# Expert routing inside the gating stage with bf16 masks, and unread products between the layers' matmuls

## The reference, cut to what matters

```python
x = x + attn(layernorm(x))            # 4 layers, width 128, hidden 512: "the layers"
x = x + xattn(layernorm(x), ctx)      # a gate per channel, from the context's greatest values: "the gating"
x = x + ffn(layernorm(x))             # 8 experts, the best 2 for each token: "routing" and "the experts"
```

```python
gate_logits = einsum('bsh,he->bse', x, gate_w)
top_vals, top_idx = top_k(gate_logits, 2)
probs = softmax(top_vals)
out = sum over the two experts e of a token: probs[e] * (x @ expert_w[e])
```

## Time and profile before

| | us |
|---|---|
| runs, median of 3 (lowest, highest) | 1199.26 (1190.36, 1199.87) |
| the profiled execution's own time | 1194.41 |
| its span, first to last instruction | 1192.4 |
| start and embedding, to the first `z` of the layers | 0 to 124.66 |
| layers, slots s = 0 to about 15 | 124.66 to 412 |
| end of the layers, gating | 412 to 615 |
| routing | 615 to 655 |
| experts | 655 to 1192 |

### The profile page before, as it was taken

How to read it: one execution, slowest core, us unless ns; L and a number is a source line. 1 busy time by engine, 2 the same in 40 slices (tenths; PEclk the granted TensorE clock), 3 DMA queues, 4 the chain that set the end, 5 groups by cost and what they waited for, 6 DMA issues and landing times. The chain is left out here.

```text
span 1192.4 us, 13599 instructions
## 1 busy us (share of the span) xinstructions
PE 1042.3 (87%) x3593; PEld 575.2 (48%) x3594; DVE 570.3 (48%) x1637; ACT 393.8 (33%) x1124; POOL 487.3 (41%) x661
## 2 busy tenths in 40 slices
PE   6786888888888869989965699999999999999995
PEld 6784454454544435425965344444444444444442
DVE  5636479788888677996965211111111111211111
ACT  2435778676756316866830000000000000000000
POOL 3834467546655201005710643333444333334431
PEclk9878899888889979988765799999999999999998
DMA  8310110110000123000795247354645636374432
GB/s 304 121 54 0 46 68 13 54 36 1 1 1 1 70 79 134 1 1 18 283 350 215 73 86 226 74 177 104 211 79 136 169 73 211 70 211 82 86 78 36
DMA packets 38462, 120.27 MB, mean 101 GB/s; under 512 B 6219, under 2 KB 9350, under 8 KB 38406
## 3 DMA queue, kind: packets, MB, share of 16 engines
q1 hardware_dynamic: 25590, 79.77, 18.1%
q0 software_dynamic: 12816, 39.86, 15.4%
HBM read 82.91 MB, written 36.70 MB: 100 GB/s over the span
## 5 line engine op out<-in xcount | busy, mean ns | idle before, releaser
L1952 PE MATMUL bank<-T,X 128*128 x1184 | 510.6, 594 | 13.9 <-DVE X L1990 10.8
L1952 PEld LDWEIGHTS bank<-T,X 128*128 128x128 f32 x1184 | 225.2, 191 | 298.6 <-issue 298.6
L2004 DVE TENSOR_SCALAR X<-bank,col_p 128x512 f32<-128x512 f32 x37 | 27.8, 750 | 410.5 <-PE bank L1952 410.5
L1970 ACT ACTIVATE X<-bank,col_p 128x512 f32<-128x512 f32 x37 | 25.4, 687 | 523.2 <-PE bank L1952 523.2
L1905 POOL DMA_INDIRECT X<-x_nrm,col_s x156 | 149.5, 958 | 92.9 <-issue 46.9
L1914 POOL DMA_INDIRECT out_dram<-X,col_d x37 | 60.0, 1622 | 268.6 <-DVE X L2004 255.0
L450 POOL TENSOR_TENSOR T<-T 128x8 f32<-128x8 f32 x216 | 94.5, 437 | 16.3
L634 PE MATMUL bank<-nat,T 128*128 128x512 f32 x128 | 88.0, 840 | 12.1 <-ACT X L787 5.4
L799 ACT ACTIVATE M<-X,T 128x256 bf16<-128x256 f32 x200 | 98.5, 497 | 0.0
L459 POOL TENSOR_TENSOR rs<-ve,neg_half 128x4 f32<-128x4 f32 x36 | 38.5, 1069 | 104.7 <-DVE ve L942 104.5
L787 ACT ACTIVATE X<-bank,T 128x512 f32<-128x512 f32 x64 | 43.8, 686 | 70.1 <-PE bank L634 69.6
(11 more groups left out here) (317 smaller groups left out, 1462.9 us busy)
## 6 DMA issues: line engine op xcount, KB each, us to landing
T<-in_L_ffn_expert_w_dram SPq DMA_DIRECT2D x8, 4096.0 KB, 17.6
out_dram<-X SPq DMA_DIRECT2D x17, 512.0 KB, 4.7
M<-in_x_dram SPq DMA_DIRECT2D x16, 512.0 KB, 7.3
X<-in_x_dram SPq DMA_DIRECT2D x16, 512.0 KB, 4.7
x_nrm<-H SPq DMA_DIRECT2D x16, 512.0 KB, 3.7
T<-in_ctx_dram SPq DMA_DIRECT2D x9, 512.0 KB, 4.0
X<-x_nrm,col_s POOLq DMA_INDIRECT x156, 3.6
X<-in_ctx_dram SPq DMA_DIRECT2D x4, 512.0 KB, 7.0
```

Of the source, the lines that this page charges most:

```text
L1952: mm = nc.tensor.matmul(bank[2 * u + n][:, :], xgt[u][:, k, :], Tf[:, ds(odd * (KD * D) + (k * D + n * BANK), BANK)], start=(k == 0), stop ...
```

## The change

**In the layers**, PE's queue gets 11 products in each of 16 slots (2 + 3 + 2 between steps as shown, 4 at the first place). Each has 512 columns of bf16; the sources are the bits of `ident` and `ones`, the target is the PSUM bank HD[0] after `hid_act` says that all four hidden results of the last visit were read. Nobody reads them.

**In the routing**, the block of its own is gone: its work is written behind the gating's on each engine, and part of it goes into the expert block, behind the first three index columns. The masks are bf16; the lane mask is built by 16 instructions of 128 elements instead of one of 2048. The prefix sum moves to DVE and PE adds the places up in PSUM. The probability is split into three bf16 pieces with products of their own, in the expert block. The first expert's load is issued at b = 4 of the gating, the second after the last store. The expert weights lie in T as two halves of each row.

```diff
@@ layers, TensorE @@
+                dense = ones[:, :].bitcast(BF16).unsqueeze(1).to_broadcast([P, 2, 2 * P])
+
+                def keep_busy(s, n):
+
+                    if 0 <= s - 1 < VISITS:
+                        pe.wait_ge(hid_act, s * FT)
+                        for i in range(n):
+                            nc.tensor.matmul(bank[HD[0]][:, :].rearrange("p (a n) -> p a n", a=2), ident[:, :].bitcast(BF16)[:, 0:P], dense, start=(i == 0), stop=(i == n - 1))
...
                     if 0 <= s - 1 < VISITS:
                         back(s - 1, 0, 2)
+                    keep_busy(s, 4)
                     if 0 <= s < VISITS:
                         var_second(s)
                     if 0 <= s - 1 < VISITS:
                         back(s - 1, 2, FT)
                     if b0 is not None:
                         fill(b0, 2 * h0)
+                    keep_busy(s, 2)
                     if 0 <= s < VISITS:
                         spread_second(s)
+                    keep_busy(s, 3)
                     if b0 is not None:
                         fill(b0, 2 * h0 + 1)
                     for p, step in prepared(s):
                         prepare(p, step)
+                    keep_busy(s, 2)
                     if 0 <= s + 3 < FINAL:
                         var_first(s + 3)
@@ gating, SP @@
+                    if b == B // 2:
+                        sp.wait_ge(back_mm, 2 * B)
+                        sp.wait_ge(l_mm, NT // 2)
+                        sp.dma_start(wslot[:, 0, :, :], expert_src(0)).then_inc(w_in_sem[0], 16)
 
                 sp.dma_start(out[N:N + P, :], X[:, 0, :]).then_inc(out_init, 16)
+                sp.dma_start(x_nrm[0:1, :], nring[0][0:1, :]).then_inc(out_init, 16)
                 sp.wait_ge(back_mm, 4 * B)
-                sp.wait_ge(l_mm, B)
-                for w in range(2):
-                    sp.dma_start(wslot[:, w, :, :], expert_src(w)).then_inc(w_in_sem[w], 16)
+                sp.wait_ge(l_mm, NT)
+                sp.dma_start(wslot[:, 1, :, :], expert_src(1)).then_inc(w_in_sem[1], 16)
@@ gating, TensorE: tile by tile, then the routing's products @@
+                    upto = CT * b if b < B - 2 else CT * b + 1 if b < B - 1 else CT * B
+                    for t in range(done, upto):
+                        second_part(t)
+                    done = upto
...
+                pe.wait_ge(r_dve, 14)
+                nc.tensor.matmul(bank[TOTAL][:, 0:E], ones[:, :], prefix[:, :, NT - 1], start=True, stop=True).then_inc(r_pe, 1)
+                nc.tensor.matmul(bank[PLACE][:, 0:NT * E], upto_neg[:, :], flat(either), start=True, stop=False)
+                nc.tensor.matmul(bank[PLACE][:, 0:NT * E], ones[:, :], flat(prefix), start=False, stop=True).then_inc(r_pe, 1)
+                for k in range(2):
+                    pe.wait_ge(hot_set, k + 1)
+                    for t in range(NT):
+                        mm = nc.tensor.matmul(bank[TOKEN][:, 0:2 * WIDE], hot_lane[k][:, t, :], of_token[k][:, t, :, :].rearrange("p a s -> p (a s)"),
+                                              start=(k == 0 and t == 0), stop=(k == 1 and t == NT - 1))
...
+                for c in range(QK):
+                    for j in range(2):
+                        mm = nc.tensor.matmul(bank[SOURCE][:, c * SLOTS:(c + 1) * SLOTS], sel[:, c, :], tok_parts[:, j, 0:SLOTS], start=(j == 0), stop=(j == 1))
@@ gating, ScalarE: before the last sequence's normed @@
+                for k in range(QK):
+                    a.copy(sel[:, k, :].rearrange("p (i b) -> p i b", i=QK), ident[:, k * QP:(k + 1) * QP].unsqueeze(1).to_broadcast([P, QK, QP])).then_inc(r_sel, 1)
+                a.copy(lane_row, iota_lane[:, :]).then_inc(r_sel, 1)
+                a.activation(tile_base, step_t[:, 0, :].unsqueeze(2).to_broadcast([P, NT, WIDE]), ACT.Copy, scale=float(QK)).then_inc(r_sel, 1)
                 for h in range(CT):
                     normed((B - 1) * CT + h)
+                act.wait_ge(r_dve, 13)
+                a.activation(e2[:, :], e2[:, :], ACT.Exp).then_inc(r_act, 1)
@@ gating, VectorE: behind the last statistics @@
-                behind(B - 1)
+                dve.wait_ge(l_mm, NT)
+                then(v.tensor_tensor(known, known, bank[P2_BANK][:, 0:NT * E].rearrange("p (t e) -> p t e", e=E), ALU.add))
                 then(v.tensor_tensor(shift, over_e(mean_all(1)), over_t(g_all), ALU.mult))
                 then(v.tensor_tensor(known, known, shift, ALU.subtract))
+                behind(B - 1)
                 then(v.tensor_tensor(logits[:, :, :], known, over_e(rs_all(1)), ALU.mult))
...
+                dve.wait_ge(r_sel, QK + 2)
+                v.tensor_copy(lane[:, :, :], lane_i[:, :, :])
                 for k in range(2):
+                    route(v.tensor_tensor(at_slot[k][:, :, 0:SLOTS], iota_slot[:, :].unsqueeze(1).to_broadcast([P, NT, SLOTS]),
+                                          slot_i[:, k, :].unsqueeze(2).to_broadcast([P, NT, SLOTS]), ALU.is_equal))
+                    v.tensor_scalar(of_token[k][:, :, 0, 0:SLOTS], at_slot[k][:, :, 0:SLOTS], tok1[:, 0:1], float(QK), ALU.mult, ALU.mult)
+                    v.tensor_tensor(of_token[k][:, :, 1, 0:SLOTS], at_slot[k][:, :, 0:SLOTS], tile_base[:, :, 0:SLOTS], ALU.mult)
                     for t in range(NT):
+                        ins = v.tensor_scalar(hot_lane[k][:, t, :], lane_row, lane[:, k, t:t + 1], None, ALU.is_equal)
+                    ins.then_inc(hot_set, 1)
+
                 dve.wait_ge(r_act, 1)
...
                 dve.wait_ge(r_pe, 3)
+                v.tensor_copy(tok_parts[:, :, 0:SLOTS], bank[TOKEN][:, 0:2 * WIDE].rearrange("p (j s) -> p j s", j=2)[:, :, 0:SLOTS]).then_inc(tok_set, 1)
+                for j in range(2):
+                    weighted(0, j)
+                dve.wait_ge(r_pe, 4)
+                route(v.tensor_scalar(src_i[:, :, :].rearrange("p s c -> p c s"), bank[SOURCE][:, 0:QK * SLOTS].rearrange("p (c s) -> p c s", c=QK),
+                                      quarter[:, 0:1], None, ALU.add))
@@ experts, TensorE: ahead of the loop @@
+                for k in range(2):
+                    pe.wait_ge(p_set, k + 1)
+                    for t in range(NT):
+                        mm = nc.tensor.matmul(bank[PROB][:, 0:3 * WIDE], hot_lane[k][:, t, :], of_prob[k][:, t, :, :].rearrange("p a s -> p (a s)"),
+                                              start=(k == 0 and t == 0), stop=(k == 1 and t == NT - 1))
@@ experts, VectorE: behind the first three sources @@
+                weighted(0, 2).then_inc(p_set, 1)
+                v.tensor_scalar(end_i[:, :], end, 1.0, None, ALU.add)
...
+                for j in range(3):
+                    ins = weighted(1, j)
+                ins.then_inc(p_set, 1)
+                turned(0, 0, 0)
+                sources(IN_FLIGHT, 0)
...
+                dve.wait_ge(p_mm, 1)
+                weigh(dve, v.tensor_reduce(pair_p[:, :], bank[PROB][:, 0:3 * WIDE].rearrange("p (j s) -> p j s", j=3)[:, :, 0:SLOTS].rearrange("p j s -> p s j"), AX.X, ALU.add))
```

More of the change, by code:

```diff
@@ L1336, in decoder_kernel, with small @@
         CNT = D * B
+        Mf = M[:, :, :].rearrange("p k n -> p (k n)").bitcast(F32)
+        xo = 0
+        def small(*shape, dt=F32):
+            nonlocal xo
+            n = 1
+            for s in shape:
+                n *= s
+            xo += n
+            assert xo <= KD * N // 2
+            flat = Mf[:, xo - n:xo]
+            names = "abc"[:len(shape)]
+            return (flat if dt == F32 else flat.bitcast(dt)).rearrange(f"p ({' '.join(names)}) -> p {' '.join(names)}", **dict(zip(names, shape)))
@@ new lines, in decoder_kernel @@
+        best = small(2, NT)
+        hot = small(2, NT, E)
+        eq = small(NT, E)
+        first = small(NT)
+        masked = small(NT, E)
+        either = small(E, NT)
+        e2 = small(NT)
+        prob = small(2, NT)
+        prefix = small(E, NT)
+        full = small(E, NT)
+        need = small(E)
+        ends = small(E + 1)
+        begin, end = ends[:, 0:E], ends[:, 1:E + 1]
+        place = small(NT, E)
+        pos_i = small(2, NT, dt=I32)
+        lane_i = small(2, NT, dt=I32)
@@ new lines, in decoder_kernel, with small16 @@
+        slot_i = small(2, NT, dt=I32)
+        lane = small(2, NT)
+        past = small(E, SLOTS)
+        who = small(SLOTS)
+        who_i = small(SLOTS, dt=I32)
+        odd_i = small(SLOTS, dt=I32)
+        ready_i = small(SLOTS, dt=I32)
+        end_i = small(E, dt=I32)
+        WIDE = SLOTS + SLOTS % 2
+        def small16(*shape):
+            n = 1
+            for s in shape:
+                n *= s
+            flat = small(n // 2).bitcast(BF16)
+            names = "abc"[:len(shape)]
+            return flat.rearrange(f"p ({' '.join(names)}) -> p {' '.join(names)}", **dict(zip(names, shape)))
@@ new lines, in decoder_kernel @@
+        lane_row = small16(P)
+        tile_base = small16(NT, WIDE)
+        sel = small16(QK, QK * QP)
```

(67 more changed lines are left out.)

221 lines of the change are left out of this document (80 added, 141 removed).

## The result

The changed kernel takes 1166.8 us (median of 4 runs, 1166.5 to 1175.4) where the kernel before took 1196.7 beside it (4 runs, 1190.4 to 1199.9): ratio 0.976 [0.973, 0.980], faster. The prediction said 1158, range 1146 to 1182. The profiled execution has a span of 1164.9 us against 1192.4, so 27.5 us have to be found.

The account below looks back on a forecast made before the run. It took PE, slowed by the lower clock, to bound the layers, and a serial routing to delay the experts' loop. Sum: 1194.4 - 18 (layers) - 19.5 (routing) + 1.0 (DMA) = 1157.9, forecast 1158 us, range 1146 to 1182.

Parts of the forecast that it names:

- Layers, -18: In the 16 layer slots, dummy products in PE's short waits keep the clock up: -18 us, against a bound of 27.
- the four slots that the prediction walked through: Layer slots at 259.87, 277.92, 297.51 and 318.15: predicted gains of 0.8, 1.5, 2.2 and 2.5 us, together 7.0.
- the 24 of the walk: Layers: the four slots' gain taken to 16 slots, 28 us, scaled to the stage's clock, 24 us.
- Routing, -19.5: Logits to last index: no common wait, cheaper bf16 masks and products; last index at 635.8 instead of 655.30, -19.5 us.
- the 1.9 taken with a view to rows 4: Routing, lane mask for each k: 16 instructions of 128 elements at 0.12 us each, 1.9 us; ends 1.3 and 5.2.
- DMA, +1.0: Second expert's load runs into the first gathers, whose landing beside a load is 4.2 us instead of 2.8: +1.0 us.
- takes the first six unread products of a slot for free or covered: Layers: four ahead of the second variance (0.9 us) free in PE's wait; two ahead of the second spread (0.4 us) mostly covered.
- taking tiles one by one reorders that work and doesn't shorten it: Gating's end: PE runs without a gap up to the last logits product at 614.5, which the new order leaves there.
- (a): Rival: the layers' clock doesn't come back and overrunning dummies cost some 5 us: 1181 us, chance 0.12.
- (b): Rival: the wait moves to DMA, early load delaying stores or second load the first gathers: 1167 us, chance 0.10.
- (c): Rival: dummies become PE's bound in the layers, 4.7 us a slot against 2.6 idle: slower, 1210 us, chance 0.03.
- (d): Rival: the unread products are dropped on the way to the chip and the layers stay: 1176 us, chance 0.03.

Follow-up runs that it names:

- five of the eleven: Changed kernel with only the last five of each slot's eleven unread products (three ahead of the second filling, two ahead of the first variance): 1167.2 us, ratio 0.976.
- the layers' part alone: The kernel before plus only the layers' unread products, without the routing changes: 1181.3 us, ratio 0.988.
- the fastest kernel: Changed kernel with the turned tail, ACT's six copies ahead of the two held tiles, one-instruction lane masks and dense products behind the logits: 1160.4 us, ratio 0.972.
- the turned tail: Changed kernel, last six tiles' gating products with the gate's 8 columns as weights, 256 tokens moving: 1164.6 us; the same without the layers' unread products: 1179.9 us.

## Why the prediction was right, and where it was off

**Layers, -18.** The mechanism is the stated one: the four slots that the prediction walked through gave 7.6 us where it said 7.0, each within 0.5. That the sum up to the last visit is 17.8 is partly luck, since the 24 of the walk was cut by a quarter on judgement, and the slots differ from 3.0 us shorter to 1.0 longer.

The time saved isn't all kept: the stretch behind the last visit, 44.48 us, takes 47.35. Of these 2.9 us, 2.0 lie ahead of the last variance, and the trace shows that they are the unread products' own. Before:

```profile
412.08 1.05 PE L582 MATMUL bank<-inv_col,nat 128*128 128x1 f32 x8 [1.50 <-ACT nat L775]
```

and after:

```profile
392.06 1.03 PE L688 MATMUL bank<-ones,ident 128*128 128x512 bf16 x4
...
394.63 1.67 PE L688 MATMUL bank<-ones,ident 128*128 128x512 bf16 x7
396.30 1.05 PE L582 MATMUL bank<-inv_col,nat 128*128 128x1 f32 x8
```

From the last `z` to this last variance (line 582) PE waits 2.3 us in all before, 1.50 of it in the row shown. After, 22 unread products of 0.215 us stand there, 4.7 us, and PE has no gap left. The last variance comes 21.65 us behind the last `z` instead of 19.66; with five of the eleven it is 19.67. The other 0.9 us are the clock: from 403.80 on PE's products stay at the lower level for some 5 us, the same ones from 419.57 on before for some 3. So the term was right as far as the last `z`. Over the stage that it was worked out for, 124.66 to 412, the gain is 15.8, and at the layers' end 14.9: there the term was 3 us too large. Another 1.4 us go before the gating's small products, with the layers' part alone as well; they were not traced further.

**Routing, -19.5.** Right within 0.5: a gain of 19.9 from the logits on (20.5 expected), and a loss of 0.9 ahead of them (1.0). Inside it two errors partly cancel: the lane mask took 2.69 us for each k instead of 1.9, inside the stated ends, and the mask products behind the second mask 1.25 instead of 1.9. On the small instructions, the estimate of 3.0 us for 16 of them from the fixed latency that the Trainium skill gives (VectorE: DVE Perf Modes, TRN2 errata) was nearer than the 1.9 taken with a view to rows 4; the trace says 2.69.

**DMA, +1.0.** The stretches behind the last index took 1.2 us more, 0.6 up to the first expert product and 0.6 in the experts. The held tiles slipped as the walk had it and were covered. The prediction called 2.8 us the landing of a gather with no load beside it; in the earlier trace rows it is the least of the gathers that do lie beside one, so the step from 2.8 to 4.2 isn't shown. Undoing the early load cost 2 to 3 us.

**The step that failed** is the price of what lies between the two parts: the sum has no term for it. It shows in two passages. One takes the first six unread products of a slot for free or covered, the four ahead of the second variance because PE waits there; behind the last `z` it doesn't wait long enough (2.0 us, above). The other is the sentence on the gating, "taking tiles one by one reorders that work and doesn't shorten it". It is right in its words, since the order of before gives the same tail, but wrong as a cost of nothing. PE works there without a gap on products of 8 columns, whose records follow each other at 0.098 us or at 0.213, and which of the two it is goes by where the clock stands and not by the order. The tail took 17.2 us before and with the layers' part alone, 20.25 with both parts. The forecast took the 10.74 us for 64 records of the earlier trace rows over as given when everything ahead of them had moved.

Between 1157.9 and the 1167.0 of the profiled execution lie 9.1 us. The ledger has 8.2 of them in these stretches: 2.9, 1.4, 0.8 and 3.1. The rest is 0.2 in the layers' term, 0.5 in the routing's and 0.2 behind the last index.

**The rivals.** (a) The clock does come back in the layers (0.97 by the windows), from 0.89. By the oscillation part of the Trainium skill (TensorE: Matmul & The Clock Gate), as the prediction read it, filling such short waits would have brought nothing; the slots at 1.00 speak against that reading. It took up only one of the two causes that the page gives; the other, short idling between groups of products, agrees with these slots. Where the clock did cost time was the gating, and no rival had that. (b) didn't happen here; a milder form of it, the first gather under the second load, holds the fastest kernel back by 1.9 us. (c) is out for the whole, though not everywhere: PE as the bound of the slot at 306.69 still made it shorter, but the unread products cost 2.0 us behind the last `z`. (d) is out: 176 of them ran.

**What stays open:** why the clock from 580 to 590 is 0.50 with one kernel and 0.71 with another that issues the same products in the same order some 1 us apart. In these runs it stayed low or alternated over small products, and in both runs with the turned tail it came back once the wide ones had begun; what decides between the first two was not found. Also open are the 1.4 us and the 0.8 us of the ledger.

## What to carry to other kernels

When a change moves everything behind it, cost the stretches in which TensorE is busy without a gap on narrow products again, at both clock levels: their price is a range, and two parts of a change needn't add up across them. Unread dense products pay where the engine waits and not where it works: count the waits at the end of a loop too, not the average slot's. Where the engine works without a gap on narrow products, turn the product round so that the real work is wide. A wait that is taken out early is worth only what the stretches up to the next bound keep of it.

## What the runs showed of the hardware

- 8-column f32 records with 128x128 weights follow each other at 0.098 us at the upper clock level and at 0.213 at the lower, so that 16 of them (a tile) are 1.6 or 3.4 us; 256-column ones with 8 columns of weights take 0.226 at the upper level, 3.62 us for two tiles.
- A 512-column bf16 product between them adds its full 0.21 us: six small records take 0.59 us, and each dense product adds 0.21 to that.
- A DVE compare of 2048 elements takes 2.29 us with f32 operands and result, and the same with a bf16 result, one bf16 operand and one f32, both broadcast; 16 of 128 elements with bf16 data take 2.69. 16 bf16 mask products of 80 columns take 1.25 us at the lower clock and 0.79 at the upper.
